# Four gated attention layers with four feed-forwards on one core: second attention's rows normalised within the first feed-forward, its bias additions in its first halves, three scatters per half behind the deviation

## The reference

```python
for l in range(4):
    x = x + tanh(g_xattn[l]) * attention_l(layernorm(x), ctx)   # 16 heads of 8, own biases; l == 1: causal mask
    x = x + tanh(g_ffn[l]) * ffn_l(layernorm(x))
# ffn_0: (silu(x @ wg.T) * (x @ wu.T)) @ wd.T, hidden 384
# ffn_1: 2 of 8 experts by router score, 1024 places each:
scores = x_flat @ router_w + router_b
top_scores, assign = top_k(scores, 2); gates = softmax(top_scores)
onehot = one_hot(assign, 8)
pos = cumsum(cumsum(onehot, axis=0), axis=1); mask = onehot * (pos < cap)
h = gelu((grouped @ w2) * (grouped @ w1)); eo = h @ w3      # token itself where no place was left
# ffn_2: block quantised, hidden 512; ffn_3: FP4 fake quantised, hidden 512
```

## Time and profile before

| what | value |
|---|---|
| median of 3 runs | 1101.15 us (1098.89 to 1103.28) |
| the profiled execution | 1099.51 us, of it 1097.4 us span |
| busy | PE 907.6 (83%), DVE 888.4 (81%), ACT 686.5 (63%), POOL 532.1 (48%) |
| granted TensorE clock | 0.894 of full speed, mean |

### The profile page before, as it was taken

How to read it: one execution, slowest core, us unless ns; L and a number is a source line. 1 busy time by engine, 2 the same in 40 slices (tenths; PEclk the granted TensorE clock), 3 DMA queues, 4 the chain that set the end, 5 groups by cost and what they waited for, 6 DMA issues and landing times.

```text
span 1097.4 us, 30165 instructions
## 1 busy us (share of the span) xinstructions
PE 907.6 (83%) x11563; PEld 712.2 (65%) x11563; DVE 888.4 (81%) x2304; ACT 686.5 (63%) x1810; POOL 532.1 (48%) x620
## 2 busy tenths in 40 slices
PE   7999999999999932999789999978899999344443
PEld 5888879978887721566458778834478888122222
DVE  4999988878899971567568888888978888899997
ACT  4888864377776610445457777856578888555553
POOL 5345402253467676223287877157653321355553
PEclk9999999999999966899889999978899999556565
DMA  8750000000000012365111111000000000000000
GB/s 215 194 223 3 2 2 1 2 2 3 2 22 26 28 45 78 110 186 173 51 33 31 31 29 28 2 1 1 1 2 3 2 2 3 1 10 15 15 15 24
DMA packets 60526, 44.42 MB, mean 40 GB/s; under 512 B 15196, under 2 KB 55781, under 8 KB 59366
## 3 DMA queue, kind: packets, MB, share of 16 engines
q1 hardware_dynamic: 55718, 34.09, 10.6%
q0 software_dynamic: 4096, 8.34, 2.5%
q10 hardware_dynamic: 576, 0.13, 0.1%
HBM read 23.73 MB, written 18.87 MB: 39 GB/s over the span
## 4 chain that ended last, share of the span: by engine, by line
PE 63%; DVE 21%; issue 6%; POOL 4%; ACT 2%; DVEq 2%; DMA 1%; another core or an unknown queue 0%; POOLq 0%; SPq 0%; ACTq 0%
PE ps L735 9%; PE ps L694 9%; PE ps L662 7%; PE ps L575 4%; PE ps L680 4%; PE ps L708 4%; PE ps L770 3%; PE ps L779 3%; PE ps L771 3%; DVE rowmax L1848 3%; PE ps L628 2%; POOL q_out L1215 2%; PE ps L643 2%; PE ps L641 2%; PE ps L585 2%
## 5 line engine op out<-in xcount | busy, mean ns | idle before, releaser
L1848 DVE TENSOR_REDUCE rowmax<-ps 128x16 f32<-128x1024 f32 x128 | 155.8, 1217 | 40.0 <-PE ps L662 38.9
L1854 DVE TENSOR_TENSOR sm<-ps,rowmax 128x512 f32<-128x512 f32 x256 | 164.9, 686 | 3.4
L1020 ACT ACTIVATE pr<-ps 128x512 f32<-128x512 f32 x256 | 139.0, 595 | 38.9 <-PE ps L735 36.7
L735 PE MATMUL ps<-cst,sm 128*128 128x128 f32 x1024 | 138.4, 276 | 12.0 <-DVE sm L1854 11.2
L694 PE MATMUL ps<-vbd,pr 128*64 128x18 f32 x4096 | 140.1, 211 | 0.5 <-ACT pr L1020 0.5
L1300 POOL TENSOR_SCALAR xn<-x_sb,mv_all,rstd_all 128x128 f32<-128x128 f32 x122 | 98.1, 804 | 76.4 <-PE ps L628 70.9
L694 PEld LDWEIGHTS ps<-vbd,pr 128*64 128x64 f32 x4096 | 134.0, 138 | 1.3 <-ACT pr L1020 1.3
L735 PEld LDWEIGHTS ps<-cst,sm 128*128 128x128 f32 x1024 | 113.1, 141 | 24.1 <-issue 18.2
L924 ACT ACTIVATE qbd<-ps,bqp,cst 128x128 f32<-128x128 f32 x256 | 104.6, 463 | 6.7 <-issue 1.9
L960 ACT ACTIVATE vbd<-ps 64x128 f32<-64x128 f32 x256 | 70.8, 277 | 35.5 <-PE ps L680 27.5
L1185 POOL DMA_INDIRECT big<-expert_out,row_g x64 | 68.2, 1065 | 48.5 <-DMA expert_out<-xn_all 23.0
(11 more groups left out here) (294 smaller groups left out, 2343.8 us busy)
## 6 DMA issues: line engine op xcount, KB each, us to landing
slots<-hT SPq DMA_DIRECT2D x8, 1024.0 KB, 12.0
sm<-slots SPq DMA_DIRECT2D x32, 256.0 KB, 3.2
expert_out<-xn_all SPq DMA_DIRECT2D x16, 256.0 KB, 2.7
ew<-in_L_ffn_w SPq DMA_DIRECT2D x24, 128.0 KB, 2.5
out<-x_sb SPq DMA_DIRECT2D x32, 64.0 KB, 1.5
slots<-xn_all,row_s POOLq DMA_INDIRECT x64
big<-expert_out,row_g POOLq DMA_INDIRECT x64
x_sb<-in_x SPq DMA_DIRECT2D x1, 512.0 KB, 4.6
```

The costliest lines, as they stand in the source:

```text
L735: last = nc.tensor.transpose(turned[b][:, r * P:(r + 1) * P], sm[x][:, c:c + P], ident)
L1020: nc.scalar.activation(pr[y][:, b, :], turned[b], ACT.Exp, scale=SCALE).then_inc(p_ready[y], 1)
L1848: v.tensor_reduce(row3, sc, AX.X, ALU.max).then_inc(rowmax_ready[x], 1)
L1854: v.tensor_tensor(sm[x][:, :].rearrange("p (r g k) -> p r g k", r=RG, k=S)[:, part], sc[:, part], row3[:, part].unsqueeze(3).broadcast_to( ...
```

## The change

POOL no longer normalises rows within the second attention. Behind each deviation of the first feed-forward it normalises that tile straight into `xn_all`, whose context is no longer needed, and counts it in a new semaphore `rows_normal`; PE turns the rows from there. POOL adds the biases to x in halves 0 to 15, two tiles each. The batches are 7, 7, 6, 6 and 6 tiles instead of 8, 8, 6, 5 and 5. The scatters stand behind the deviation, up to three in a half, without the waits on DVE's subtraction and PE's scores. Two semaphores of loads are merged into one (`late_weights_in`), and `normalised(k)` corrects the counts of `xn_ready` for the stage that no longer raises it.

```diff
-BATCHES = ((0, 8), (8, 16), (16, 22), (22, 27), (27, 32))
+BATCHES = ((0, 7), (7, 14), (14, 20), (20, 26), (26, 32))
...
+    def normalised(k):
+        return IT * (k - 1 if k > ATTENTION_STAGE[1] else k)
...
-                        if later is not None:
-                            pe.wait_ge(xn_ready[x], IT * k + later + 1)
+                        if later is not None and l == 1:
+                            u = later * NS + x
+                            pe.wait_ge(rows_normal, u + 1)
+                            nc.tensor.transpose(turned[0][:, T_XN], xn_all[:, u * D:(u + 1) * D], ident).then_inc(xnT_psum[x], 1)
+                        elif later is not None:
+                            pe.wait_ge(xn_ready[x], normalised(k) + later + 1)
                             nc.tensor.transpose(turned[0][:, T_XN], xn[x][:, :], ident).then_inc(xnT_psum[x], 1)
...
-            def scattered(t):
-                u = t - (BATCHES[0][1] - 1 + ROUTE + 4)
-                if not 0 <= u < T or t >= T + 3:
-                    return None
-                return next(b for b, (first, end) in enumerate(BATCHES) if first <= u < end), u
+            def scatters():
+                done, n = {}, 0
+                for t in range(T + 3):
+                    done[t] = []
+                    while len(done[t]) < 3 and n < 2 * T:
+                        b = next(b for b, (first, end) in enumerate(BATCHES) if n // 2 < end)
+                        if BATCHES[b][1] - 1 + ROUTE + 4 > t:
+                            break
+                        done[t].append((b, n // 2, n % 2))
+                        n += 1
+                left = [(b, u, c) for b, (first, end) in enumerate(BATCHES) for u in range(first, end) for c in range(2)][n:]
+                return done, left
...
-                    if l == 1 and scattered(t) is not None:
-                        if prev is not None:
-                            pool.wait_ge(sm_ready[y], subtracted(l, prev))
-                        scatter(*scattered(t), 0)
+                    if l == 1:
+                        rows = None
+                        for u in range(NS * t, min(NS * t + NS, T)):
+                            xt = x_sb[:, u * D:(u + 1) * D]
+                            nc.gpsimd.tensor_tensor(xt, xt, y_bias_b[l][:, :], ALU.add).then_inc(x_biased[u % NS], 1)
...
-                    if l == 1 and scattered(t) is not None:
-                        if new is not None:
-                            pool.wait_ge(s_psum[x], IT * l + new + 1)
-                        scatter(*scattered(t), 1)
...
                     if oldest is not None and l == 1:
                         rstd(k, oldest, y)
+                    for b, u, c in scattered[t] if l == 1 else ():
+                        scatter(b, u, c)
...
                     if older is not None:
                         rstd(k, older, x)
-                        u = NS * (older + 3 - IT) + x - 1
-                        if 0 <= u <= NS:
-                            normal_rows(1, u)
+                        u = older * NS + x
+                        if then is not None:
+                            pool.wait_ge(xn_ready[x], IT * k + then + 1)
+                        pool.wait_ge(rstd_ready[x], IT * k + older + 1)
+                        nc.gpsimd.tensor_scalar(xn_all[:, u * D:(u + 1) * D], x_sb[:, u * D:(u + 1) * D], mv_all[:, 2 * u:2 * u + 1], rstd_all[:, u:u + 1],
+                                                ALU.subtract, ALU.mult).then_inc(rows_normal, 1)
...
-            for b, (first, end) in enumerate(BATCHES):
-                for u in range(max(first, scattered(T + 2)[1] + 1), end):
-                    if u == T - 2:
-                        pool.sem_inc(scatters_late, 1)
-                    for c in range(2):
-                        scatter(b, u, c)
+            for b, u, c in scattered_after:
+                if u == T - 2 and c == 0:
+                    pool.sem_inc(scatters_late, 1)
+                scatter(b, u, c)
```

33 lines of the change are left out of this document (17 added, 16 removed).

## The result

| | before | changed | ratio (95% interval) |
|---|---|---|---|
| median of 4 runs each | 1100.02 us (1097.94 to 1103.28) | 1114.65 us (1112.26 to 1117.38) | 1.0127 (1.0101 to 1.0153) |
| profiled execution, span | 1097.4 us | 1114.4 us | |

The change makes the kernel 1.3% slower, where I forecast 1092.6 us with a range of 1088 to 1101. The measured median lies 13.7 us above the upper end of the range, and the time moved the other way.

What follows compares the result with a forecast made beforehand. Bounds: PE in the first feed-forward, PE and DVE by turns in the second attention, then scatters. Halves -2.7 feed into last scatters -7.0, then experts' start -8.5; normalisation zero: 1101.15 - 8.5 = 1092.6 us, range 1088 to 1101.

Steps and rivals of the forecast that it cites:

- Normalisation in the feed-forward, at zero: First feed-forward: POOL's 32 normalisations of 0.80 us fit into halves of 2.12 us and cost nothing.
- The third rival: First feed-forward: POOL's normalisation holds DVE's L1512, +14 us, 1106.7 us, slower; chance 10%.
- Halves of the attention, -2.7: Second attention: L1581 back at 0.34 us (-3.2), smaller batches -0.3, a moved routing piece +0.8; bounds -3.7 and +4.
- less comes through: Rival: halves with scatters stay stretched, experts gain only the four scatters, about -4 us, 1097 us; chance 17%.
- The last scatters, -7.0: Behind the second attention: start 1.9 us earlier, four scatters fewer (-5.1), last ends at 424.9; bounds -4 and -8.
- The start of the experts, -8.5: First expert's matmul (L770): starts 8.5 us earlier, the middle between 7.0 and 9.9 us.
- a slow stretch of DVE's loop: Ahead of the experts: turns of 8.4 us; if it stays, DVE moves 7.0 us, if gone, PE starts 9.9 earlier.

Runs made afterwards that it cites:

- e_none: The changed kernel with no scatter within the second attention, all 64 left for behind it; one run, 1146.31 us.
- e_three_op: The changed kernel, three scatters a half behind the deviation, with an idle power of one column on POOL between each two; ratio to before 0.9955.
- e_three_op_again: The same kernel as e_three_op, measured once more on another chip; ratio to before 0.9954.
- e_before_again: The kernel before, unchanged, measured once more against itself; ratio 1.0007.
- e_two_op: The changed kernel with two scatters a half instead of three and an idle power of one column on POOL between them; one run, 1099.67 us.
- e_two_op_timed: The same kernel as e_two_op, now timed, on another chip; ratio to before 1.0030.
- e_two_landed: The changed kernel with two scatters a half, the second waiting until the first has landed, no operation between them; one run, 1101.38 us.

## Why the prediction was wrong

**Normalisation in the feed-forward, at zero: right.** The changed kernel's timeline there, DVE and POOL:

```profile
205.74 0.56 DVE L1782 SCALAR_TENSOR_TENSOR hid<-ps,gate_both 128x384 f32<-128x384 f32 x1 [0.21 <-ACT gate_both L980]
...
207.86 0.56 DVE L1782 SCALAR_TENSOR_TENSOR hid<-ps,gate_both 128x384 f32<-128x384 f32 x1 [0.21 <-ACT gate_both L980]
...
208.59 0.39 DVE L1530 TENSOR_SCALAR xn<-x_sb,mv_all,rstd_all 128x128 f32<-128x128 f32 x1
...
212.83 0.34 DVE L1530 TENSOR_SCALAR xn<-x_sb,mv_all,rstd_all 128x128 f32<-128x128 f32 x1
...
208.10 0.80 POOL L1368 TENSOR_SCALAR xn_all<-x_sb,mv_all,rstd_all 128x128 f32<-128x128 f32 x1 [0.18 <-POOL rstd_all L1186]
...
212.63 0.80 POOL L1368 TENSOR_SCALAR xn_all<-x_sb,mv_all,rstd_all 128x128 f32<-128x128 f32 x1 [0.18 <-POOL rstd_all L1186]
```

The distance of the hidden rows is 2.12 us, as in the earlier trace rows, and DVE's L1530 (L1512 before) takes 0.34 us where it starts 0.20 us into POOL's normalisation (L1368) and 0.39 where it starts 0.49 us into it, with 0.60 and 0.31 us of that still to run. The third rival is refuted. The Trainium skill (SBUF — State Buffer, section "SBUF: two separate sides") has the rule on which the third rival was argued: of two that want the shared ports, one waits "for the whole instruction". For this pair the trace does not agree, since L1530 is never held by more than 0.12 us over the stage; L1610 and L1611 beside the additions, above, do look held to the addition's end.

**Halves of the attention, -2.7: the step that failed.** The working said: three scatters and the deviation are 4.4 us on POOL, below 4.73, so they are harmless, at most +4. POOL was indeed never short; it idled. What failed is that the working put the effect of adjacent scatters on PE's semaphores at nothing. They rise up to 3.5 us late, which costs 1.1 to 2.3 us against e_none in eleven of the fifteen halves, and the attention from the first to the 32nd row maxima became 17.1 us longer where I had 2.7 shorter. The terms themselves mostly held: L1599 (L1581 before) is at 0.34 us in every half of the changed kernel, and with gaps between the scatters first to 32nd row maxima take 151.73 us (e_three_op) for 154.24 in before, on different chips, and 153.05 (e_three_op_again) for 154.57 (e_before_again) on one chip: -2.5 and -1.5 against the -2.7 forecast. My mistake was to price a scatter by its own length on POOL. In the trace of before no two scatters stood together while PE worked: in the attention they start at least 2.1 us apart up to half 31, by just those waits and operations that the change takes from between them; one pair is in the earlier trace rows, 333.98 and the next at 336.10. (In the last three halves pairs stand 1.34 us apart, and PE has little left to do there.) But a hint lay there: PE's signals behind single scatters rise up to 0.8 us late in that trace, and the prediction looked at DVE's operations alone. The rival "less comes through" comes nearest, but for another reason (stretched operations of DVE), and it stood 4.5 us above the forecast, where the result is 22 above.

**The last scatters, -7.0: size roughly right, start missed.** The changed kernel's POOL and the first expert:

```profile
415.63 0.58 POOL L1186 TENSOR_TENSOR rstd_all<-mv_all,cst 128x1 f32<-128x1 f32 x1 [2.42 <-DVE mv_all L1851]
417.67 1.04 POOL L1210 DMA_INDIRECT slots<-xn_all,row_s  x1 [1.46 <-DVE row_s L1636]
...
447.22 0.97 POOL L1210 DMA_INDIRECT slots<-xn_all,row_s  x1 [0.30 <-issue]
...
459.24 2.05 PE L779 MATMUL ps<-q_r,ew 128*128 128x512 f32 x2 [1.45 <-DVEq L1977]
```

24 scatters from 417.67 to 448.19, 30.5 us, as worked out. But the first starts 2.0 us behind the last deviation, for 0.8 in the kernel before (395.66 and 396.42): it waits for the fourth batch's rows (L1636), which I had put ahead of it. In e_three_op the last one ends 196.9 us behind the first row maxima for 202.4 before, -5.5 for -7.0.

**The start of the experts, -8.5: -6.0 with gaps.** From the first row maxima to the first expert's matmul e_before_again has 214.4 us and e_three_op_again, on the same chip, 208.4. (Before has 213.9 and e_three_op 206.1, but on different chips.) I took the middle between a slow stretch of DVE's loop that stays (-7.0) and one that goes (-9.9). Both happen: on the chip of e_three_op the last thirty additions, fifteen turns, run in 11.21 us with no break, and PE's first L780 waits for ACT alone; on the chip of e_three_op_again the stretch is there, with idle times of 5.31 us. e_two_op, too, has it on one chip and not on the other. All three traces of the chip of e_three_op have no slow stretch, and all others have it. So it is neither the number of scatters nor their place that decides, and what does I can't say.

With the stall taken away the change gives 0.9954 or 0.9955, some 5 us of the 8.5 forecast.

**What stays open.** How such scatters delay what PE raises is not shown: only at which distances, by how much, and that what DVE and ACT raise passes meanwhile. The Trainium skill (Perfetto Trace Analysis, section "DMA Instruction — SWDGE (GPSIMD)") says that the end of such a row is the end of writing descriptors and not of moving data. This case's traces agree: a row ends 1.0 us behind its start, the landing comes 2.3 us behind it (e_two_op_timed), and a scatter that waits for that landing starts 3.1 us or more behind it (e_two_landed). In the half shown of the changed kernel the engines restart 1.7 to 1.9 us behind the last scatter's start, so before it lands. Why the same kernel shows late signals in one execution and none in another (e_three_op and its repeat, on two chips) is open too. And e_two_op_timed at 1.003 stays unexplained. Of the 8.5 us that its span has over e_three_op's, 3.2 are the start, 3.5 lie between there and the first expert's sum and 1.9 behind it, but the kernel before left no trace on that chip to hold beside them.

## What to carry to other kernels

An operation that is "hidden" on an idle engine can still hold up the others: before waits between two such operations are removed, look for a place in the trace where they already stand together beside the work that they would meet, and if there is none, keep the upper bound wide. When every engine is idle at once and the releasers ended long ago ("remote"), compare the end of each releasing instruction with the time at which its semaphore rose, and tabulate the restart against the rows of all other engines; here it stood at a nearly fixed distance behind a scatter. Here an idle operation of 0.6 us between adjacent scatters, three a half, was worth some 19 us, and one of 0.2 us between two was worth 0.7: the distance between two starts is what to design for, and it has to be measured rather than guessed from the length of a row.

## What the runs showed of the hardware that I had not expected

- Where an indirect scatter of POOL starts 1.34 to 1.43 us behind another, what PE raises counts late, by up to 2.1 us with two of them and 3.6 with three; it comes through about 1.6 us behind the start of the second (1.8 behind that of the third). Where it starts 1.75 us or more behind, PE's signals are late by at most 1.1 us, and in some executions not at all.
- PE's own matmuls slow only with three adjacent ones: sixteen take up to 1.9 us in the changed kernel for 0.73, and at most 0.80 with two.
- A scatter lands 2.3 us behind its start, and one that waits for that landing starts 3.1 us or more behind it, though the row is 1.0 us long.
- DVE operations with two SBUF operands that start 0.03 to 0.15 us into one of POOL's additions took 0.38 to 0.50 us for 0.22; beside POOL's deviation they did not.
- The moment at which TensorE's clock rises at the start parts two executions of one kernel by up to 1.6 us, and all traces by up to 4.4 us.
- One kernel's loop on DVE has a slow stretch on one chip and none on another.
